# Second attention: the next keys' tile normalised behind the low parts of keys and query in every step

## The reference, cut to what matters

```python
x = _layernorm(features, gm, bm)            # 512 context rows
lat = _layernorm(latents, gl, bl)           # 512 rows of x
q = (lat @ Wq) ...                          # 16 heads of 64
kv_input = jnp.concatenate([x, lat], axis=1)
k = (kv_input @ Wk) ... ; v = (kv_input @ Wv) ...
sim = jnp.einsum('bhqd,bhfd->bhqf', q * SCALE, k)
sim = sim - jnp.max(sim, axis=-1, keepdims=True)
out = jnp.einsum('bhqf,bhfd->bhqd', softmax(sim), v) ...
return out @ Wo
```

## Time and profile before

| | us |
|---|---|
| median of three runs | 3398.57 |
| the profiled execution's own time | 3397.3 |
| its span, first to last instruction | 3395.7 |
| PE busy | 3141.2 (93%) |
| DVE busy | 2206.5 (65%) |
| POOL busy | 1656.1 (49%) |
| ACT busy | 1342.6 (40%) |

### The profile page before, as it was taken

One profiled execution on the slowest core, in us unless ns is written; L12 is line 12 of the kernel. 1 busy time (PEld: TensorE's weight loads), 2 busy tenths in 40 slices (PEclk: granted clock), 3 DMA queues, 4 the chain that ended last, 5 costly groups with the idle time before them and its releaser, 6 DMA issues. The chain is left out here.

```text
span 3395.7 us, 58842 instructions
## 1 busy us (share of the span) xinstructions
PE 3141.2 (93%) x18285; PEld 2302.8 (68%) x18286; DVE 2206.5 (65%) x5104; ACT 1342.6 (40%) x2058; POOL 1656.1 (49%) x1001
## 2 busy tenths in 40 slices
PE   5885999999879999999999999999999977879978
PEld 4655788888756666666666666666666656679966
DVE  5667455555657777777777777777776663245545
ACT  2332333333334444444444444444444432234422
POOL 5002333333236666666666666666665655770047
PEclk7995999999989999999999999999999977989999
DMA  4000000001111111212121112121211032342253
GB/s 114 1 0 1 20 14 9 14 10 59 78 57 60 66 60 40 78 47 81 38 62 62 63 38 80 45 84 35 66 62 51 11 110 81 131 156 72 72 179 104
DMA packets 118349, 204.62 MB, mean 60 GB/s; under 512 B 13793, under 2 KB 85545, under 8 KB 112433
## 3 DMA queue, kind: packets, MB, share of 16 engines
q1 hardware_dynamic: 105200, 173.30, 15.2%
q0 software_dynamic: 12992, 29.72, 3.0%
HBM read 141.28 MB, written 61.64 MB: 60 GB/s over the span
## 5 line engine op out<-in xcount | busy, mean ns | idle before, releaser
L2281 POOL TENSOR_TENSOR d_acc<-d_acc,d_pr 128x1024 f32<-128x1024 f32 x384 | 936.9, 2440 | 90.8 <-ACT d_pr L2135 60.4
L2135 ACT ACTIVATE d_pr<-d_p 128x1024 f32<-128x1024 f32 x512 | 487.3, 1026 | 239.7 <-PE d_p L2062 239.4
L1995 PE MATMUL d_pO<-d_pr,d_V 128*64 128x512 f32 x2048 | 473.0, 599 | 0.0
L2281 POOL TENSOR_TENSOR d_acc<-d_pr 128x1024 f32<-128x1024 f32 x64 | 153.3, 2395 | 625.1 <-ACT d_pr L2135 625.1
L2191 DVE TENSOR_REDUCE d_nm<-d_p 128x2 f32<-128x1024 f32 x256 | 303.8, 1221 | 87.6 <-PE d_p L2038 87.6
L942 POOL TENSOR_TENSOR e_hs<-e_hf,e_hs 128x512 fp32r<-128x512 f32 x136 | 175.7, 1292 | 365.1 <-ACT e_hs L917 365.1
L2186 DVE CUSTOM_DVE_ANT_0 d_biased<-d_p,d_masked 128x512 f32<-128x512 f32 x512 | 330.5, 688 | 28.1 <-issue 28.1
L1995 PEld LDWEIGHTS d_pO<-d_pr,d_V 128*64 128x64 f32 x2048 | 135.4, 136 | 261.5 <-issue 234.7
L972 DVE SCALAR_TENSOR_TENSOR res<-e_pY,m_Wt,res 128x256 f32<-128x256 f32 x544 | 225.9, 478 | 44.9 <-PE e_pY L878 44.1
L2202 DVE RECIPROCAL d_rb<-d_rb 128x128 f32<-128x128 f32 x256 | 224.6, 920 | 9.3 <-ACT d_rb L2128 9.3
L963 DVE TENSOR_TENSOR e_hf<-e_sl,e_pU 128x512 f32<-128x512 f32 x136 | 93.7, 689 | 209.2 <-ACT e_sl L914 209.2
(11 more groups left out here) (333 smaller groups left out, 5868.2 us busy)
## 6 DMA issues: line engine op xcount, KB each, us to landing
d_W<-w_split SPq DMA_DIRECT2D x30, 1536.0 KB, 6.8
d_masked<-mask_bias SPq DMA_DIRECT2D x64, 256.0 KB
kv_split<-d_parts SPq DMA_DIRECT2D x56, 256.0 KB
d_kv<-kv_split SPq DMA_DIRECT2D x7, 2048.0 KB
x_slots<-m_zeros SPq DMA_DIRECT2D x1, 9088.0 KB
b_x<-x_slots SPq DMA_DIRECT2D x71, 128.0 KB
y_slots<-b_y SPq DMA_DIRECT2D x71, 128.0 KB
xh_split<-m_XH SPq DMA_DIRECT2D x8, 1024.0 KB
```

The source lines that it names most:

```text
L1995: last = pe.matmul(pO[own[h], :], V[vb][:, s, par * P + h * HD1:par * P + (h + 1) * HD1], pr[:, s % PT, h, :], start=(s == 0), stop=(s == ...
L2135: act.activation(pr[:, n % PT, :, :], slot(st, what, n)[:, :, :], ACT.Exp).then_inc(exp_done, 1)
L2281: pool.tensor_tensor(acc[:, q, :, :], a, pr[:, s % PT, :, :], ALU.add).then_inc(acc_done, 1)
```

## The change

In the even list X goes from the front (ahead of M, KK and Q) to behind KK and Q. In the odd list X goes from between Q and KK to behind VV0, ahead of den and S0. Only DVE has an instruction for X, so on DVE the order becomes: even steps YY (of the step before), KL, QL, X, S0 instead of YY, X, KL, QL, S0; odd steps QL, KL, X, S0 instead of QL, X, KL, S0. Nothing else moves, and the work is the same.

```diff
 WHOLE = (
-    """X M KK Q ST0 ST1 ST2 S0 S1 PV0 PV1 S2 ST3 S3 den PV2 PV3 S4 ST4 r0 ST5 r1 r2 ST6 ST7 S5 PV4 r3 PV5 PV6 PV7 O
+    """M KK Q X ST0 ST1 ST2 S0 S1 PV0 PV1 S2 ST3 S3 den PV2 PV3 S4 ST4 r0 ST5 r1 r2 ST6 ST7 S5 PV4 r3 PV5 PV6 PV7 O
        S6 S7 T YY N Z""".split(),
-    """Q X KK M VV0 den S0 ST0 ST1 S1 ST2 ST3 ST4 ST5 ST6 r0 ST7 r1 r2 S2 r3 PV0 PV1 PV2 PV3 S3 S4 S5 PV4 PV5 PV6 PV7
+    """Q KK M VV0 X den S0 ST0 ST1 S1 ST2 ST3 ST4 ST5 ST6 r0 ST7 r1 r2 S2 r3 PV0 PV1 PV2 PV3 S3 S4 S5 PV4 PV5 PV6 PV7
        S6 S7 T VV1 N Z O YY""".split())
```

## The result

The changed kernel takes 3551.11 us (four runs, 3550.57 to 3553.06), the kernel before, run beside it, 3398.84 us (four runs, 3397.33 to 3399.88). The ratio is 1.0451, with a 95% interval of 1.0439 to 1.0464: slower by 152 us, where 5.2 were forecast and the range ended at 3409.5.

The account below looks back on a forecast made before the run. PE was taken to bound the kernel, DVE counting only where PE waits for it. Even steps +6.3, odd steps +0.3 and -1.4 made +5.2 us on 3398.6: 3403.8 us, range 3397.5 to 3409.5.

Parts of the forecast that it names:

- X costs one and the same thing wherever it stands: On DVE, X takes 2.82 us to the next unit's start in any place, overlapping the unit ahead by 0.08 us.
- The 1.00 us by which S0 was to be late: Even steps on DVE: X's 2.82 less 0.08 of overlap less 1.74 idle puts S0 and S1 1.00 us later.
- ST3 with 0.10 us left: Even steps on PE: ST3 waits for S0's maxima, which even 1.00 us later leave 0.10 us, so nothing is lost.
- S3 0.21 us late in 28 steps: Even steps on PE: S3 waits for S1's maxima and starts 0.21 us late, 5.9 us over 28 steps.
- the stop inside X: Every fourth even step: a 0.16 us stop that may stay with X, at most 1.1 us in all, taken as 0.4.
- The even term, 6.3: All even steps together: S3's lateness, 5.9 us, plus 0.4 for X's stop, +6.3 us.
- Odd steps: Odd steps: +0.3 us for S0's possibly later maxima, -1.4 us for KL coming earlier after the loop's jump.
- Rival 1: Even steps: S3 is not held up and only KL's lead stays, 3397.2 us; chance 0.14.
- Rival 2: Every step: DVE's register operations ahead of S0, 0.24 us, come on top of X's end, 3415.0 us; chance 0.09.
- Rival 3: Odd steps after the loop's jump: the 0.97 us stop in X delays S0 to 10.5 us, 3409.1 us; chance 0.13.

Follow-up runs that it names:

- e2: Kernel before with only the odd list changed, X behind VV0, even list as it was: 3391.95 us, ratio 0.9984.
- e5: Changed kernel plus a wait: in even steps GpSimd's first addition waits until X has ended; 3406.28 us, ratio 1.0033 to the kernel before.
- e4: Changed kernel with X's Newton steps as tensor_scalar with one tensor operand and its last instruction cut into 255 and 1 columns: 3454.86 us, ratio 1.0172 to the kernel before.
- e8: Changed kernel, but in the even list X stands between KK and Q: 3468.89 us, ratio 1.0204 to the kernel before.
- e6: Changed kernel plus 15 idle matmuls on PE ahead of ST3 in even steps: 3513.71 us, ratio 1.0352 to the kernel before.

## Why the prediction failed, point by point

**The step that failed** is "X costs one and the same thing wherever it stands". It was read off one place in the odd steps and used as a constant. Beside an idle GpSimd X lasts 2.9 us, or up to 3.2 with its short stop (before, e2, e5). When an addition catches only its last, wide instruction it lasts 4.5 (e4, whose X is 3.4 by itself) or 4.9 (e8); when two of its instructions are caught, 6.7 (a Newton step and the last) or 7.4 (two Newton steps). The forecast took a duration from a row without asking what ran on the other engines at that time, nor what would run there in the new place. The 1.00 us by which S0 was to be late was 4.8 (14.44 against 9.64).

**ST3 with 0.10 us left, "nothing lost".** As arithmetic it holds: in e5, with X at its old length, ST3 isn't held up in 21 of the 28 steps (in the seven with the stop it is, by 0.15). With 4.8 us on DVE it was the first to wait, came 3.71 to 4.37 us late, and took S3's place as the bound.

**S3 0.21 us late in 28 steps.** Confirmed by e5 in 21 steps, at 0.20. Two things were too small: the 0.10 us behind the wait was left out (2.8 in all), and the stop inside X, priced at 0.4 and at most 1.1, stays in seven steps at 0.26 us each (1.8). The even term, 6.3, measured 10.9 there (a stage of +9.3, plus what the odd steps gained, 1.6). So with X at its old length the sum would still have come out some 4 us low, though inside the range.

**No term for the clock.** The forecast had PE at a granted clock of 1.00 and no wait long enough to ask about it. Each of the 28 waits (3.54 us in 21 steps, 4.20 in seven) cost 1.7 us more (half of 3.41), 47.8 in all, of which e6 gave back 34.0.

**Odd steps.** Forecast -1.1 (+0.3 and -1.4), measured -2.1. KL at 5.55 us and the memset at 9.55 came as written. Behind the loop's jump the gain is larger than the estimate.

**The rivals.** Rival 1 (S3 not held up) is refuted by e5, in which it is held up by the amount forecast. Rival 2 (exposed register operations) was priced at 0.24 us a step; in e5 S3 would have been 0.45 late, and was 0.20. In step 9 of e2 DVE shows 0.19 us of "issue" ahead of S0, so it exists there, in a place with room. Rival 3 (the stop now hits S0) didn't come: S0's memset is at 9.79 us of step 9 in e2 (9.74 in the changed kernel), not 10.5, and the stop is gone from X. By the rule of the Trainium skill that was weighed there (Advanced Engine Details and Errata, section ISA Cache) the fetch would still have fallen in X; these runs neither show nor rule out that it now passes in DVE's idle time. None of the rivals was about a neighbour of X, and so none of them came near the time.

## What to carry to other kernels

Before moving a unit on VectorE, lay GpSimd's timeline beside the old and the new place, and look at the shortest and the longest duration of each VectorE instruction with two inputs in SBUF: where one shape takes 0.69 to 2.80 us, compare its ends with GpSimd's; and an instruction that never varies may only stand in the other's idle time. A chain of tiny instructions is a bad thing to bring there, since each can be held for nearly a whole GpSimd instruction, as two in a row were here; if it must go there, make GpSimd wait for it (e5), shorten GpSimd's instructions, or use a form with one tensor operand on a single column (e4). And where a wait of PE grows from nothing to 4 us, price the clock behind it too.

## What the runs showed of the hardware

- Of this chain a scalar_tensor_tensor on a single column, 0.16 us of work, lasts 2.21 us when held. A tensor_scalar on a single column, with the other operands as scalars from SBUF, was not held (e4: 212 to 276 ns, 336 of them, 91 of which ran wholly inside a GpSimd addition); one on 255 columns was (1.50 us).
- GpSimd is held in turn: in the kernel before, 21 of its additions take 2.85 to 2.90 us instead of 2.39, and beside each of them a product L2206 of DVE, which started 0.02 to 0.07 us ahead, keeps its 0.69 us. Between GpSimd's two additions in step 12 after the change there is 0.08 us (1343.67 to 1343.75), as between most of its additions in a row; DVE's next instruction met the second one, so two in a row were held.
- VectorE's masked reductions of the scores, with one of two operands in PSUM, were not held: in the kernel before 512 of them took 679 to 693 ns, 299 of them wholly inside a GpSimd addition.
- PE's waits of 3.54 and 4.20 us after the change were each followed by 3.41 us at the 1.2 GHz level. Behind shorter waits for the same maxima this came in some steps only: in one of 28 behind 1.31 us (e4, step 2, which took 28.68 us instead of 27.05), and in seven of 28 behind 1.72 us (e8, where they took 28.7 to 29.2 us instead of 27.47).
